# Splitting a group's summed slots into two float32r parts before they are placed, in a three-layer GCN kernel

## The reference

```
deg  = segment_sum(ones, dst);  dinv = rsqrt(deg);  norm = dinv[src] * dinv[dst]
conv(h, W, b) = segment_sum((h @ W)[src] * norm, dst) + b
out = layernorm(x + conv(conv(conv(x, W1, b1), W2, b2), W3, b3))      (all float32)
```

## Time and profile before

| | |
|---|---|
| profiled execution | 2390.54 us |
| its span in the trace | 2388.7 us |
| busy: PE / PEld / DVE / ACT / POOL | 2012.8 / 1092.5 / 1358.8 / 754.5 / 1663.6 us |
| mean granted TensorE clock | 0.941 of full speed |
| gathers L969 | 1698, from 137.8 to 2346.5 us, 1635.1 us busy |
| placing matmuls L1194 | 288 instructions, 172.0 us busy |
| slot copies L1485 | 144, 84.2 us busy |
| group adds L1903 | 288, 202.8 us busy |

### The profile page before, as it was taken

How to read it: one execution, slowest core, us unless ns; L and a number is a source line. 1 busy time by engine, 2 the same in 40 slices (tenths; PEclk the granted TensorE clock), 3 DMA queues, 4 the chain that set the end, 5 groups by cost and what they waited for, 6 DMA issues and landing times.

```text
span 2388.7 us, 31641 instructions
## 1 busy us (share of the span) xinstructions
PE 2012.8 (84%) x9902; PEld 1092.5 (46%) x9902; DVE 1358.8 (57%) x3393; ACT 754.5 (32%) x1445; POOL 1663.6 (70%) x1746
## 2 busy tenths in 40 slices
PE   6665778999889987888899898997799999999863
PEld 6321224444444432345555555554455655555421
DVE  8425765666666653254444444445555666555677
ACT  0602543444344432232223222223322223222211
POOL 0257777777777777477777777777577777777772
PEclk9867989999999999999999999999899999999986
DMA  7556887888888888578888888889788888888894
GB/s 276 216 166 189 269 276 228 248 246 248 254 272 274 256 247 249 167 223 242 241 236 251 243 253 261 265 263 306 204 246 254 254 249 259 271 277 280 275 309 156
DMA packets 283058, 591.28 MB, mean 248 GB/s; under 512 B 72467, under 2 KB 125648, under 8 KB 282896
## 3 DMA queue, kind: packets, MB, share of 16 engines
q0 software_dynamic: 136624, 446.62, 61.9%
q1 hardware_dynamic: 146272, 142.67, 18.0%
HBM read 523.67 MB, written 65.45 MB: 247 GB/s over the span
## 4 chain that ended last, share of the span: by engine, by line
POOL 30%; issue 10%; PE 8%; DMA 7%; DVE 2%; DVEq 0%; ACT 0%; ACTq 0%; POOLq 0%
POOL ring L969 30%; DMA ring<-y_dram,kept 5%; PE ps L1295 4%; PE ps L1183 2%; DMA out_dram<-row_sb 2%; PE ps L1194 1%; DVE row_sb L1972 0%; PE ps L1348 0%; DVE acc L1903 0%; DVE ln L1958 0%; DVE h_sb L1949 0%; DVE h_sb L1956 0%; DVEq L1899 0%; DMA y_dram<-acc 0%; DVE acc L2100 0%
## 5 line engine op out<-in xcount | busy, mean ns | idle before, releaser
L969 POOL DMA_INDIRECT ring<-y_dram,kept x1698 | 1635.1, 963 | 581.3 <-issue 503.4
L1183 PE MATMUL ps<-ring,onehot 128*32 128x512 f32 x3396 | 479.3, 631 | 165.0 <-DMA ring<-y_dram,kept 163.6
L2100 DVE SCALAR_TENSOR_TENSOR acc<-ps,acc 128x512 f32<-128x512 f32 x442 | 304.9, 690 | 301.9 <-PE ps L1295 289.5
L1295 PE MATMUL ps<-dense_first,wide_a 128*128 128x512 f32 x1020 | 296.5, 413 | 13.5 <-DVE dense_first L2071 6.4
L1876 DVE TENSOR_TENSOR onehot<-ps,kept 128x128 f32<-128x128 f32 x429 | 122.8, 287 | 249.8 <-PE ps L1183 248.5
L1903 DVE SCALAR_TENSOR_TENSOR acc<-ps,mask,acc 128x512 f32 x288 | 202.8, 746 | 78.8 <-issue 73.0
L1295 PEld LDWEIGHTS ps<-dense_first,wide_a 128*128 128x128 f32 x1020 | 190.5, 193 | 117.8 <-issue 53.4
L1295 PE MATMUL ps<-dense_next,wide_a 128*128 128x512 f32 x730 | 221.3, 412 | 10.5 <-ACT wide_a L1536 10.5
L1183 PEld LDWEIGHTS ps<-ring,onehot 128*32 128x32 f32 x3396 | 73.5, 109 | 338.4 <-issue 332.4
L1295 PE MATMUL ps<-dense_first,y_rows 128*128 128x512 f32 x680 | 203.8, 422 | 0.6
L1194 PE MATMUL ps<-onehot 128*128 128x512 f32 (+1 forms) x288 | 172.0, 681 | 28.8 <-issue 14.3
(11 more groups left out here) (286 smaller groups left out, 2128.9 us busy)
## 6 DMA issues: line engine op xcount, KB each, us to landing
ring<-y_dram,kept POOLq DMA_INDIRECT x1698, 4.8
onehot<-a_dram SPq DMA_DIRECT2D x408, 64.0 KB
y_dram<-acc SPq DMA_DIRECT2D x99, 256.0 KB, 9.9
a_dram<-ring SPq DMA_DIRECT2D x17, 784.0 KB, 5.6
acc<-in_x_dram SPq DMA_DIRECT2D x1, 12288.0 KB
y_dram<-acc SPq DMA_DIRECT2D x12, 1024.0 KB, 10.8
out_dram<-row_sb SPq DMA_DIRECT2D x48, 256.0 KB
w_sb<-in_x_dram SPq DMA_DIRECT2D x24, 256.0 KB
```

The costliest lines, as they stand in the source:

```text
L969: pool.indirect_dma_start(ring[:, s, :], None, y_dram[layer], bass.IndirectOffsetOnAxis(ap=rows, axis=0)).then_inc(done, 16)
L1183: mm = pe.matmul(ps[k * WIDE:(k + 1) * WIDE, g % BANKS, :], wide_hot[:, r, k, :], ring[:, r * CPQ + k, :], start=opens, stop=closes, tile_ ...
L1295: mm = pe.matmul(ps[:, bank, :], wide_slots[n % WIDE_SLOTS][:, P * k:P * (k + 1)], y_parts[(TILES * (layer - 1) + tile) % YSLOTS][:, part, :],
L2100: dve.scalar_tensor_tensor(out=rows, in0=ps[:, UNIT_BANKS[n % len(UNIT_BANKS)], :], scalar=0.5, in1=rows, op0=ALU.mult, op1=ALU.add).then_ ...
```

## The change

ScalarE's copy now writes the rounded (float32r) part of a group's slots, in one buffer and not two in turn. VectorE gets a new instruction for each of the 144 groups, `split_slots`: it waits for that copy and writes bank minus copy, the low part. It stands at the end of VectorE's work for the quad that closes the group. TensorE places the two parts with two float32r matmuls that accumulate, in place of one fp32 multiplication. A slot bank is free, and a group may be placed, after `split_slots`; ScalarE's copy of group g waits until group g-1 has been placed (before: g-2). The one-hot of the placing is written as float32r. The number of dense tiles stays at 17.

```diff
-        place_hot = small[:, hots_at:hots_at + 2 * P].rearrange("p (b n) -> p b n", b=2)
+        place_hot = place_rows[:, 0:2 * P].rearrange("p (b n) -> p b n", b=2)
-        slots = small[:, slots_at:slots_at + 2 * D].rearrange("p (b d) -> p b d", b=2)
+        slots_high, slots_low = place_rows[:, 2 * P:2 * P + D], place_rows[:, 2 * P + D:2 * P + 2 * D]
...
                 if opens and g >= BANKS:
-                    pe.wait_ge(slots_copied, g - BANKS + 1)
+                    pe.wait_ge(slots_split, g - BANKS + 1)
...
                 pe.wait_ge(place_ready, g + 1)
-                pe.wait_ge(slots_copied, g + 1)
+                pe.wait_ge(slots_split, g + 1)
                 if g > 0:
                     pe.wait_ge(added, 2 * g)
-                pe.matmul(ps[:, PLACE_BANK, :], place_hot[0:rows, g % 2, :], slots[0:rows, g % 2, :],
-                          start=True, stop=True).then_inc(placed, 1)
+                pe.matmul(ps[:, PLACE_BANK, :], place_hot[0:rows, g % 2, :], slots_high[0:rows, :], start=True, stop=False)
+                pe.matmul(ps[:, PLACE_BANK, :], place_hot[0:rows, g % 2, :], slots_low[0:rows, :],
+                          start=False, stop=True).then_inc(placed, 1)
...
-                if g >= 2:
-                    act.wait_ge(placed, g - 1)
-                act.copy(slots[0:rows, g % 2, :], ps[0:rows, g % BANKS, :]).then_inc(slots_copied, 1)
+                if g >= 1:
+                    act.wait_ge(placed, g)
+                act.copy(slots_high[0:rows, :], ps[0:rows, g % BANKS, :]).then_inc(slots_copied, 1)
...
+            def split_slots(g):
+                rows = LAST_ROWS if own_of(g) == GROUPS - 1 else P
+                dve.wait_ge(slots_copied, g + 1)
+                dve.tensor_tensor(slots_low[0:rows, :], ps[0:rows, g % BANKS, :], slots_high[0:rows, :].bitcast(F32),
+                                  ALU.subtract).then_inc(slots_split, 1)
...
                     for tile in splits_at(layer, q):
                         low_part(layer, tile)
+                    if n + 1 == QUADS_TO[g]:
+                        split_slots(g)
...
                     build(q)
+                    if q + 1 == QUADS_TO[g]:
+                        split_slots(g)
                     for k in splits0_at(q):
                         low0(k)
```

More of the change, by code:

```diff
@@ L334, in gcn_three_layers_resnorm @@
         y0_rows = sb("y0_rows", [P, 4, D], F32R)
-        sb("below_dense", [P, STORE_QUADS * CPQ * P - y_words], F32)
+        sb("below_slots", [P, RING_QUADS * CPQ * WIDE], F32)
+        place_rows = sb("place_rows", [P, 2 * P + 2 * D], F32R)
+        sb("below_dense", [P, STORE_QUADS * CPQ * P - RING_QUADS * CPQ * WIDE - 2 * P - 2 * D - y_words], F32)
         dense_last = sb("dense_last", [P, y_words], F32R)
@@ L562, in gcn_three_layers_resnorm @@
         slots_copied = sem("slots_copied")
+        slots_split = sem("slots_split")
         place_ready = sem("place_ready")
```

## The result

The changed kernel takes 2399.03 us (median of 20 runs, 2389.33 to 2403.8); the kernel before, run beside it 20 times, 2389.33 (one of these 20 took 4757.65 us and is no part of the ratio). The ratio is 1.004, 95% interval 1.0028 to 1.0053: 9.6 us slower, 6.7 to 12.7. That is 0.4%: within the bound that the prediction set for no change, though with this many runs the interval leaves out zero. The forecast was 7.6 us slower. The changed kernel's profiled execution took 2396.65 us (span 2394.8, mean clock 0.935), against 2390.54 (2388.7, 0.941) before: 6.1 us.

What follows compares the result with a forecast made beforehand. GpSimd's gather queue bounds the kernel, then VectorE's list from about 2255 us. Layer ends 1.3 + 0.6, norm stretch 5.4 and last groups 0.3 sum to 7.6 us over 2393.7: about 2401 us, range 2385 to 2424.

Steps and rivals of the forecast that it cites:

- The bound: From 137.8 to 2346.5 us: a queue of 1698 GpSimd gathers at about 1.25 us, never held by TensorE beyond 0.3.
- rival A: Dense layers: TensorE bounds them after all; if half of the 84 us saved showed, 2352 us; 4%.
- TensorE's saving: Placings of all 144 groups: 0.58 us saved each, 84 us of TensorE, worth nothing while gathers are the queue.
- The split outside the stretch: VectorE's new subtraction in ordinary dense quads: 0.69 us each, hidden in idle time, cost 0; upper bound 99 us.
- Gathers slowed: Gathers beside the new subtraction: no slowing, as one operand is in PSUM; 0, at most 0.39 us per group.
- rival D: Gathers beside the new subtraction: half of the 144 slow them by 0.39 us each, 28 us more, 2429 us; 6%.
- Layer ends: Ends of layers 0 and 1: the split delays the last placing, +1.3 and +0.6 us.
- The norm stretch: VectorE's list, groups 136 to 141: 4.1 own time plus 0.5 and 0.8 round trip, 5.4 us, bounds 3 and 10.
- The last two groups: Groups 142 and 143: the split in front of a shorter placing, +0.3 us, -0.5 to +1.5.
- Rival B: Last eight groups: shorter placing and lighter TensorE outweigh the split, store waits take it up; 2390 us; 13%.
- Rival C: Norm stretch: the split ties TensorE to VectorE, 21 us more than the saving allows, 2417 us; 15%.
- Rival E: Placings: the float32r pair takes as long as fp32, adding only about 3 us, 2404 us; 3%.

Runs made afterwards that it cites:

- The pair alone: Changed kernel without the split, both float32r matmuls reading the high part, low part left out: 2384.44 us, 5.0 us faster than the kernel before.
- the pair of experiments: Changed kernel with one more subtraction for groups 0 to 129, from PSUM or with both operands in SBUF: 2403.58 and 2421.78 us.
- the work alone: Changed kernel executing all splits, but TensorE places the whole fp32 copy with one matmul, waiting only for the copy: 2389.88 us, +2.4 over before.
- the early split: Changed kernel with the split moved ahead of the quad's norm for groups 136 to 143 only: 2394.88 us, +5.7 over before.
- the long placing: Changed kernel, TensorE still waiting for the full split, but placing a whole fp32 copy with one fp32 matmul: 2405.01 us, +14.6 over before.
- the order alone: Changed kernel with a split of only 8 of 512 columns, TensorE waiting for it, both matmuls reading the high part: 2393.86 us, +1.0 over before.
- the early split of all groups: Changed kernel with the split moved ahead of the norm or bias for all groups of layers 1 and 2: 2397.96 us, +9.8 over before.

## Why the prediction was right, step by step

- **The bound.** Right: the gathers' queue is untouched, the saving of TensorE became waiting, and no wait for TensorE before 2255 us exceeds 0.3. The pair alone at 5.0 us faster refutes rival A. One reading was too short: the view of the earlier trace rows also has 1.7 us of waits for ScalarE's square root, which are the same in both kernels.
- **TensorE's saving.** Mis-sized. I took 0.24 us for each matmul, from sixteen of them in a row. A lone pair starts its matmuls 0.31 apart (999.82, 1000.13) and the last lasts 0.39, so 0.70 in place of 1.12. The busy time fell by 44.9 us, not 84. And it isn't worth nothing: 5 us, both without the split (-5.0) and with it (14.6 - 9.6 = 5.0, from two intervals that overlap). I gave it about 1, in the last groups.
- **The split outside the stretch: 0.** Right: 130 more of them cost 1.6 us. Its duration was forecast at 0.69 and is 0.684.
- **Gathers slowed: 0.** Right; rival D is refuted by the pair of experiments, and the row on which it stood, 1.33 us beside an instruction with two SBUF operands, was a real effect of the other kind of instruction. The Trainium skill (SBUF — State Buffer, Who interferes with whom) holds as inferred that tensor_tensor doesn't hinder descriptor generation; 1.10 in place of 0.95 us beside it, and 18 us more, decide against that. The same section states that a VectorE instruction with two SBUF inputs contends with a GpSimd instruction that reads SBUF; a gather takes its row numbers from `kept` in SBUF, and these figures agree with it. Its rule for at most one SBUF input agrees with both kernels (963 and 964 ns).
- **Layer ends: 1.3 + 0.6.** 1.4 and 0.35 to 1.0 in the traces, 2.3 by experiment. The first gathers of layers 1 and 2 did not come later, as forecast, but earlier, at 1017.7 and 1685.5 us in place of 1019.4 and 1686.9, which the forecast had named as a sign of rival A. It was a poor test: in the second profile of the changed kernel they are at 1015.6 and 1684.5, and with the work alone at 1012.4 and 1679.6. Absolute positions scatter by more than the effect; the distances within a layer end don't.
- **The norm stretch: 5.4.** 6.2 by its length in one pair of traces, 7.0 by the means of three and four, 5.1 by experiment (1 to 9). I took 4.1 of own time, which holds, and 1.3 of round trip, which is 3.1 to 4.0 in four traces. The step that failed is the placing at the low clock: I took 0.6 to 1.1 for it behind 0.14, and it is 1.2 from the first start to the last end (2343.37 to 2344.56) behind 0.11. And the cover in front of it is not 0.69 + 0.28 but 0.79, as the two overlap the split and each other. That leaves 0.54 where I had 0 to 0.3, and 1.14 where I had 0.8. The norms behind groups 136 to 141 came later by 1.26, 0.95, 1.19, 0.82, 2.08 and 1.34 us than the one before each: five within the 0.7 to 1.5 that I named, and group 140 over it. These are 7.6 us, of which the norms between gave 1.5 back. Waits for stores are 1.2 us shorter, but they scatter by 2.7 between traces, so it isn't shown that the splits are what shortens them.
- **The last two groups: 0.3.** 0 in the trace.
- **The sum** came out 2.0 us under what was measured. Its paths were right, and the round trip alone, sized about 2 us too small, would account for that. But the measured 9.6 is known only to 3 us either way, so that it came so near is in part luck.
- **Rival B** is right that the shorter placing is worth something (5 us) and wrong that it outweighs the split; that store waits take the split up isn't shown. **Rival C** names the mechanism that the early split shows, tying TensorE to VectorE, at 5 us in the stretch and 12.2 with the long placing, not at 21 more than the saving. **Rival E** is refuted by the 0.31 us between the pair's matmuls.

Open: half of the 5.0 us that the pair alone gains; 3.5 of the 6.0 us that the order alone costs; and why the early split of all groups gains nothing. Also, the order alone at +1.0 and the change at +9.6 differ by the split's own time alone, 8.6 us, while the work alone costs 2.4: a split costs more where TensorE waits for it. The traces place about 5 of the 8.6 (the stretch 117.3 and 119.5 us, the layer ends 0.75 and 0.5, the last two groups 17.7 and 19.2); the rest isn't shown.

## What to carry to other kernels

A matmul made cheaper by splitting its operand gets a second producer in front of it. Where the engine that splits is the one that later waits for the matmul, count the round trip: the time from the split's end to the matmul's end, less what that engine has to do meanwhile, at the clock that holds there. If it has little to do, move the split up: here that gave 5 us back when only the groups of the stretch were moved, and nothing when all were, for a reason not found. And before adding work to an engine at a stretch that it bounds, look at its own waits: here a second result row was worth 9.3 us without any change to the arithmetic.

## What the runs showed of the hardware

- A VectorE subtraction of 128x512 takes 0.68 us with one operand in PSUM or with both in SBUF, but only the second adds to the gathers beside it (in the case shown 1.10 us against 0.95; over 130 of them 13.6 us more of gathers, 18 us of time).
- A lone pair of float32r matmuls of 32x512 takes 0.70 us from start to end at full clock (999.82 to 1000.52). One of 128x512 in the stretch, where the granted clock is 0.79 from 2300 to 2345 us, takes 1.2, the two fp32 instructions before 2.05:

```profile
2300.00:2345.00 45.00, 22.96 (x104) 11.62 (x105) 35.76 (x82) 6.52 (x18) 34.49 (x35) 0.79 0.92 301
```

(columns as in the earlier trace rows.) TensorE is busy 22.96 of these 45 us, 6.57 less than before, at a clock that is down from 0.81 to 0.79.
